# Whole 4 MB weight strips and one output tile at a time in the two big projections of an eight-core transformer layer

## The reference

```python
x = x + attn(layernorm(x))     # q = x@wq; k = x@wk; v = x@wv; causal softmax(q k / sqrt(128)) v; out @ wo
# second half, on x' = layernorm(x):
logits = x' @ W_router.T ; w = top-2 softmax weights over 8 experts
h = einsum('td,erd->ter', x', lora_A)
x = x + x' @ W_base.T + b_base + einsum('ter,eor,te->to', h, lora_B, w) * 2.0
```

## Time and profile before

| what | us |
|---|---|
| three runs | 4990.17, 5107.53, 5207.92 |
| their median | 5107.53 |
| profiled execution | 4992.11 |
| its span, slowest core (3) | 4990.3 |
| spans of the eight cores | 4944.2 to 4990.3 |
| first P4 weight transfer issued to first P4.5 read issued | 3183.10 to 3945.17, 762.1 |
| first P5 strip transfer issued to end | 4194.31 to 4990.3, 796.0 |

### The profile page before, as it was taken

One profiled execution on the slowest core, in us unless ns is written; L12 is line 12 of the kernel. 1 busy time (PEld: TensorE's weight loads), 2 busy tenths in 40 slices (PEclk: granted clock), 3 DMA queues, 4 the chain that ended last, 5 costly groups with the idle time before them and its releaser, 6 DMA issues.

```text
span 4990.3 us, 53555 instructions; the slowest of 8 cores (4944.2 to 4990.3 us)
## 1 busy us (share of the span) xinstructions
PE 3283.9 (66%) x16530; PEld 1520.3 (30%) x16530; DVE 1951.6 (39%) x3513; ACT 1796.4 (36%) x2024; POOL 159.5 (3%) x182
## 2 busy tenths in 40 slices
PE   3555555778787887878777777746655315646764
PEld 3455554332222222222222222222322212222322
DVE  4555554046556565656566777300000121000000
ACT  3555554036556565656556767300000020000000
POOL 0000000000000000000000000000000000000000
PEclk9888888999899999999898888877877657878887
DMA  6444443640111101110100000254444442444443
GB/s 181 158 164 166 165 165 104 62 38 9 18 18 18 18 9 17 18 18 9 17 9 1 1 1 1 41 98 88 84 94 89 116 93 32 87 94 82 87 90 77
DMA packets 260879, 328.70 MB, mean 66 GB/s; under 512 B 147712, under 2 KB 218496, under 8 KB 251264
## 3 DMA queue, kind: packets, MB, share of 16 engines
q0 software_dynamic: 212800, 106.97, 17.9%
q1 hardware_dynamic: 47808, 218.33, 13.0%
HBM read 398.66 MB, written 33.55 MB: 87 GB/s over the span
## 4 chain that ended last, share of the span: by engine, by line
PE 47%; DVE 25%; DMA 10%; issue 9%; ACT 7%; DVEq 1%; SPq 1%; ACTq 0%; POOL 0%; POOLq 0%
PE qps L633 10%; PE yps L708 9%; PE y2ps L989 9%; DVE at_tp L300 8%; PE vps L552 4%; DMA xsst<-xkv 4%; DMA x2r<-x2scr 4%; DVE at_sacc L323 4%; PE at_sps L242 3%; DVE at_tq L307 3%; DVE at_tr L308 3%; PE at_ppv L282 2%; PE ptx L505 2%; PE kps L566 2%; ACT xnTq L517 2%
## 5 line engine op out<-in xcount | busy, mean ns | idle before, releaser
L265 ACT ACTIVATE at_uring<-at_sps,bias 128x1024 bf16<-128x1024 f32 x896 | 945.5, 1115 | 42.2 <-DVE at_tp L300 33.0
L282 PE MATMUL at_ppv<-at_uring,Vs 128*128 128x512 bf16 x2304 | 706.0, 389 | 328.6 <-DVE at_uring L295 320.8
L242 PE MATMUL at_sps<-qT,kTs 128*128 128x512 bf16 x2304 | 698.7, 386 | 122.5 <-ACT at_uring L260 51.9
L708 PE MATMUL yps<-wost,qT 128*128 128x512 bf16 x2048 | 462.2, 390 | 271.1 <-DVE x2st L730 257.8
L989 PE MATMUL y2ps<-wbst,xnT 128*128 128x512 bf16 x2048 | 460.9, 389 | 265.7 <-DVE x3st L1034 252.7
L300 DVE TENSOR_TENSOR at_tp<-at_uring 128x512 bf16<-128x512 bf16 x1152 | 489.6, 425 | 298.4 <-ACT at_uring L260 175.3
L633 PE MATMUL qps<-xnT,wqbf 128*128 128x512 bf16 x2048 | 532.6, 426 | 41.1 <-issue 27.6
L552 PE MATMUL vps<-wkvbf,xnTq 128*128 128x128 bf16 x2048 | 216.6, 301 | 371.6 <-ACT Vs L575 347.8
L199 DVE RECIPROCAL at_sinvb<-at_sden 128x512 f32<-128x512 f32 x64 | 214.6, 3353 | 523.2 <-ACT at_sden L193 523.2
L282 PEld LDWEIGHTS at_ppv<-at_uring,Vs 128*128 128x128 bf16 x2304 | 214.7, 97 | 637.1 <-issue 400.9
L708 PEld LDWEIGHTS yps<-wost,qT 128*128 128x128 bf16 x2048 | 204.2, 100 | 530.1 <-issue 301.1
(11 more groups left out here) (97 smaller groups left out, 2218.3 us busy)
## 6 DMA issues: line engine op xcount, KB each, us to landing
xst<-xkv SPq DMA_DIRECT2D x64, 2048.0 KB, 9.6
wqbf<-wq POOLq DMA_DIRECT2D x32, 1024.0 KB, 12.1
wost<-wo POOLq DMA_DIRECT2D x64, 512.0 KB, 5.6
wbst<-wbT POOLq DMA_DIRECT2D x64, 512.0 KB, 5.5
xsst<-xkv SPq DMA_DIRECT2D x64, 256.0 KB, 3.3
x2scr<-x2st SPq DMA_DIRECT2D x64, 256.0 KB, 2.3
x2rd<-x2scr SPq DMA_DIRECT2D x8, 2048.0 KB, 8.2
x2r<-x2scr SPq DMA_DIRECT2D x64, 256.0 KB, 3.4
```

Source lines behind the costliest of these rows:

```text
L242: ins = t.matmul(sps[bi % 2][:, (jj - j0) * 512:(jj - j0 + 1) * 512], kT[:, jj * 128:(jj + 1) * 128], qslice(g, k), start=True, stop=True)
L265: ins = s.activation(u_t(gj, b), sps[bi % 2][:, 0:b * 512], AF.Exp, bias=bias10[:], scale=SCALE)
L282: ins = t.matmul(ppv[ei % 2][:], V[:, jj * 128:(jj + 1) * 128], u_t(gj0 + jj), start=(jj == 0), stop=(jj == nj - 1))
L708: ins = t.matmul(yps[tt][:], rawT4[:, tt, ic * 128:(ic + 1) * 128], wost[gq % 3][:, ic4:ic4 + 1, :].rearrange("p a n -> p (a n)"), start=( ...
```

## The change

Both big projections turn their loops inside out. A strip's weights come as one transfer of [128, 32, 512] (4 MB as bf16, 8 MB read) into one of two strip buffers. In P4 the two buffers are the two halves of `xnT`, which is not read between the last query projection and P4.5. In P5 they are two new tiles `ws5` on the right; to make room, `kT` and `V` are released after attention and most small tiles of P5's first part are released before its second. Then, for each row tile, one tensor event runs all 32 chunks (in P5 the bias and the low-rank matmul too, 34) into one of only four PSUM banks, and waits for the strip's transfer and for the add four tiles back. A tile's add now waits for that tile's matmuls alone. A strip's transfer waits for the last matmul event two strips back. The residual loads, the adds and the stores keep their form and their order on SP and DVE. P4.5's first copies into `xnT` also wait for the last P4 matmul. `xn2T` is another name for `xnT`.

P4 (P5 has the same form):

```diff
-        wost = [p4.enter_context(nc.sbuf_tensor(f"wost{i}", [128, 4, 512], BF16, side="right")) for i in range(3)]
+        ws4 = [xnT[:, i * 16384:(i + 1) * 16384].rearrange("p (q o) -> p q o", q=32)
+               for i in range(2)]
...
-        yps = [p4ps.enter_context(nc.psum_tensor(f"yps{i}", [128, 512], F32)) for i in range(8)]
+        NB4 = 4
+        yps = [p4ps.enter_context(nc.psum_tensor(f"yps{i}", [128, 512], F32)) for i in range(NB4)]
...
         for os_ in range(8):
-            for icq in range(8):
-                gq = os_ * 8 + icq
-                w = []
-                if gq >= 3:
-                    pq = gq - 3
-                    w.append(ev_ymm[(pq // 8, (pq % 8) * 4 + 3)])
-                ev_wo[(os_, icq)] = sched.event("gpsimd", ... wost[gq % 3][:] <- wo piece ...)
-                for ic4 in range(4):
-                    ic = icq * 4 + ic4
-                    w = [ev_wo[(os_, icq)]]
-                    if ic == 0 and os_ >= 1:
-                        w.extend(ev_yev[(os_ - 1, tt)] for tt in range(8))
-                    def em_y(t, ic=ic, ic4=ic4, gq=gq):
-                        for tt in range(8):
-                            ins = t.matmul(yps[tt][:], rawT4[:, tt, ic * 128:(ic + 1) * 128],
-                                wost[gq % 3][:, ic4:ic4 + 1, :]..., start=(ic == 0), stop=(ic == 31))
+            w = []
+            if os_ >= 2:
+                w.append(ev_ymm[(os_ - 2, 7)])
+            else:
+                w.extend(p3t_tensor)
+            ev_w4[os_] = sched.event("gpsimd", lambda g, os_=os_: g.dma_start(
+                    ws4[os_ % 2], wor[:, :, os_ * 512:(os_ + 1) * 512]), ...)
             for tt in range(8):
                 j = os_ * 8 + tt
+                w = [ev_w4[os_]]
+                if j >= NB4:
+                    w.append(ev_yev[((j - NB4) // 8, (j - NB4) % 8)])
+                def em_y(t, os_=os_, tt=tt, j=j):
+                    for ic in range(32):
+                        ins = t.matmul(yps[j % NB4][:], rawT4[:, tt, ic * 128:(ic + 1) * 128],
+                            xnT[:, (os_ % 2) * 16384 + ic * 512:(os_ % 2) * 16384 + (ic + 1) * 512],
+                            start=(ic == 0), stop=(ic == 31))
+                    return ins
+                ev_ymm[(os_, tt)] = sched.event("tensor", em_y, waits=w)
...
-                w = [ev_ymm[(os_, 31)], ev_xs[(os_, tt)]]
+                w = [ev_ymm[(os_, tt)], ev_xs[(os_, tt)]]
```

More of the change, by code:

```diff
@@ L685, in build_nc @@
         ev_x2w = {}
+        p3t_tensor = [e for e in p3_tail if e.sem == "tensor"]
         for os_ in range(8):
-            for icq in range(8):
-                gq = os_ * 8 + icq
-                w = []
-                if gq >= 3:
-                    pq = gq - 3
-                    w.append(ev_ymm[(pq // 8, (pq % 8) * 4 + 3)])
[L693 to L699, removed]
-                for ic4 in range(4):
-                    ic = icq * 4 + ic4
-                    w = [ev_wo[(os_, icq)]]
-                    if ic == 0 and os_ >= 1:
-                        w.extend(ev_yev[(os_ - 1, tt)] for tt in range(8))
-                    def em_y(t, ic=ic, ic4=ic4, gq=gq):
-                        for tt in range(8):
[L708 to L714, removed]
@@ L741, in build_nc @@
         qscope.close()
+        xn2T = xnT
         p45 = contextlib.ExitStack()
@@ L947, in build_nc @@
         p5ps1.close()
+        p5m.close()
         p5b = contextlib.ExitStack()
-        wbst = [p5b.enter_context(nc.sbuf_tensor(f"wbst{i}", [128, 4, 512], BF16, side="right")) for i in range(3)]
+        ws5 = [p5b.enter_context(nc.sbuf_tensor(f"ws5_{i}", [128, 32, 512], BF16, side="right")) for i in range(2)]
         wbstb = [p5b.enter_context(nc.sbuf_tensor(f"wbstb{i}", [128, 512], BF16, side="right")) for i in range(2)]
@@ L967, in build_nc @@
         for os_ in range(8):
[L968 to L994, removed]
             w = []
             if os_ >= 2:
-                w.append(ev_b5d[os_ - 2])
+                w.append(ev_y2[(os_ - 2, 7)])
+            ev_w5[os_] = sched.event(
+                "gpsimd",
+                lambda g, os_=os_: g.dma_start(
+                    ws5[os_ % 2][:], wbr[:, 0:32, os_ * 512:(os_ + 1) * 512]),
+                waits=w, inc=16, sem=f"c_wb{os_ % 2}")
+            w = []
+            if os_ >= 2:
+                w.append(ev_y2[(os_ - 2, 7)])
             ev_wb1[os_] = sched.event(
@@ L1001, in build_nc, with em_y2 @@
                 waits=w, inc=16, sem=f"c_wbb{os_ % 2}")
[L1003 to L1017, removed]
-            ev_lora[os_] = sched.event("tensor", em_lora, waits=[ev_b5, ev_hw, ev_bb])
             for tt in range(8):
                 j = os_ * 8 + tt
+                w = [ev_w5[os_], ev_wb1[os_]]
+                if j == 0:
+                    w.extend([ev_hw, ev_bb, ev_oc])
+                if j >= NB5:
+                    w.append(ev_y2ev[((j - NB5) // 8, (j - NB5) % 8)])
+                def em_y2(t, os_=os_, tt=tt, j=j):
+                    for dc in range(32):
+                        t.matmul(y2ps[j % NB5][:],
+                                 xn2T[:, dc * 1024 + tt * 128:dc * 1024 + (tt + 1) * 128],
+                                 ws5[os_ % 2][:, dc:dc + 1, :].rearrange("p a n -> p (a n)"),
+                                 start=(dc == 0), stop=False)
+                    t.matmul(y2ps[j % NB5][:], onechunk[:], wbstb[os_ % 2][:],
+                             start=False, stop=False)
+                    return t.matmul(y2ps[j % NB5][:], h_wT[:, tt * 128:(tt + 1) * 128],
+                                    bbf[:, os_ * 512:(os_ + 1) * 512],
+                                    start=False, stop=True)
+                ev_y2[(os_, tt)] = sched.event("tensor", em_y2, waits=w)
                 w = []
```

92 lines of the change are left out of this document (53 added, 39 removed).

## The result

| what | us |
|---|---|
| kernel before, median (lowest) of its ten runs | 5002.94 (4990.17) |
| changed kernel, median (lowest to highest) of its ten runs | 4441.17 (4436.96 to 4708.73) |
| ratio to the kernel before, 95% interval | 0.8882, 0.8871 to 0.8894 |
| forecast | 4418, range 4380 to 4650 |
| profiled execution used below | 4439.93, span 4438.4 |

The change makes the kernel 11.2% faster. The forecast was 23 us under the median.

A forecast was written before the change was run, and what follows sets the result against it. The bound was taken as the exposed latency of eight loads and adds between strips. Lead-in, matmuls and tail gave P4 479.0 and P5 505.3 us, saving 573.8 from 4992.1: 4418 us, range 4380 to 4650.

The forecast's parts named there:

- What bounds the kernel: P4 and P5: PE pauses 257.8 and 252.7 us for eight serial residual loads and adds after all banks fill.
- The streams: Matmuls without pauses, 0.216 us apart: 445.4 us in P4 and 471.7 in P5, cold starts saved.
- The tails: End of P4 and P5: only the last tile's drain, add, issue and store remain, 3.6 us each.
- The lead-ins: Start of P4 and P5: the first matmul waits for a whole strip, taken as 30 us in each stage.
- my bounds of 24.7 and 44.7: Lead-in limits in us: strip alone at 209 GB/s, or landing together with the second strip, each plus 4.6 to start.
- the 36 us: Lead-in worked out from the two `wqbf` transfers, where the first came at 0.8 of the whole.
- The add chain: P4 and P5 adds: 7.5 us a step while a strip lands, 3 us of lag, costed at nothing.
- The rival in which this chain sets the pace: Every load and add step takes 7.5 us, 51 us come back: 4469 us; chance 0.06.
- The clock: Rival: the clock does not hold in the unpaused P4 and P5 streams; at 0.90, 102 us more, 4520; chance 0.13.
- the 218 us: Spread of the three earlier runs, highest above lowest, added to 4418 for the range's upper side: 4636.
- The rivals of late strips: P4 and P5 strips land partly late, 65 us each: 4595, chance 0.05; or set the end, 98.4 us each: 5129, 0.03.
- the last two: Rivals: strips set the end, slower by 2.7%, 5129 us, chance 0.03; restructuring moves nothing, 4992 us, chance 0.01.

The follow-up runs named there:

- barrier_late: Changed kernel with 8 banks and the old add waits, each later strip issued only after the adds of the strip whose buffer it takes: 5043 to 5046 us, ratio 1.0078.
- prefetching kernel: Changed kernel with P4's first two strips issued during attention and P5's first during P4's last strip: median 4375.41 us, ratio 0.8757 to the kernel before.
- barrier: Changed kernel with 8 banks and the old waits (adds wait for the strip's last tile, next strip for all adds): 5179.8 and 5188.7 us, ratio 1.0378.

## Why the prediction was right, and what it missed

**What bounds the kernel: right.** The pauses were the serial adds behind the full set of banks. Putting the old waits back, with the strips kept out of the pauses, costs 603 us (barrier_late). Transfer size and loop order bring nothing by themselves: with them and the old waits the kernel is no faster than before.

**The streams: right.** P4's matmuls run from 3221.40 to the last add's start less 0.3, 450.7 us against 445.4 forecast, of which 4.2 are waits for adds. P5's take 472.1 against 471.7. The spacing of 0.216 us read from P2 holds with 32 and 34 matmuls in a row, through every strip border.

**The tails: right.** P4's is 3675.22 - 3672.39 = 2.8 us after the last add's start, plus 0.3 of drain, where 3.6 was forecast; P5's last 4.6 us, from the end of its matmuls to the end, are 1 us over.

**The lead-ins: the mis-sized term.** 30 us forecast for each stage, 38.7 and 41.3 measured on the slowest core. That is 20 of the 23 us. Both lie inside my bounds of 24.7 and 44.7, but the reasoning between them failed: I took the rate of 209 GB/s from core 3 without looking at what its neighbour did just then, and charged the excess to the core's own second strip alone. The runs show that two neighbouring cores loading together write some 160 GB/s each (157 on core 0 in 3190 to 3221, 159 on core 1 in 3186 to 3205). At that rate 4.19 MB take 26 us, 31 with the 4.6 to start, and this is when the slowest core had them (31.2). The lower rate beside a loading neighbour, a cause that the forecast did not have, thus explains 6.5 us over the 24.7; by the reckoning under the held-back strips most of it is the neighbour's first strip, which the run with the second strips held back left in place. The other 7.5 us, in which 1.2 MB of the second strip were written too, may be the own queue after all: the 36 us that I worked out for such a pair from the earlier trace rows, and then went below, was the nearer figure. In the kernel before, core 2 had issued its three pieces (1.5 MB) at 3175.40, 8 us ahead, and its rate was down from 202 GB/s in 3182 to 3184 to 57 in 3184 to 3190, so the two hardly met. With 4 MB each, 31.2 us of writing on core 0, they did.

The rest: P4's matmul waits and spacing add 5 us, and the stretch between the stages took 245.3 us instead of 249.1. So P4 and P5 came 26 us over the forecast, and 4 us of that came back by luck, in a stretch costed as unchanged.

**The add chain: right in price, wrong in size.** I gave a step 7.5 us while a strip lands, and 3 us of lag in all. The chain on core 0 shows the loads of three tiles in a row, and steps of 12.2, 9.4 and 7.7 us between the adds:

```profile
3336.89 0.70 DVE x2st L731
...
3338.07 10.90 DMA xsst<-xkv
3349.13 0.70 DVE x2st L731
3350.31 8.08 DMA xsst<-xkv
3358.55 0.70 DVE x2st L731
3359.73 6.39 DMA xsst<-xkv
...
3366.28 0.70 DVE x2st L731
```

Against 6.9 us for a tile that is 8.7 us of lag, three times what I said, and DVE waited for a load before 51 of 64 adds. It stayed free because the banks hold it and the loads of the later tiles take 3 to 5 us. The rival in which this chain sets the pace was nearer than 0.06 suggests in mechanism, but worth only 4 us here. In the prefetching kernel, where a strip lands in P4's last strip too, the same lag shows at the stage's end and costs 8 us there.

**The other rivals.** The clock held in this profile: all eight cores have 1.00 in 3240 to 3640, inside streams of 445 and 472 us. It did not in the execution of 4708.73 us (see the last section), which lies above the range, as that of 4662.97 does: the 218 us that I allowed for such a run, read from the kernel before, were too few. That rival was costed at two prices: 4520 is worked out from the 0.90 of the earlier trace rows; the higher one in the range rests on no row and no run. What the runs showed in its place is 1.00 on all eight cores in 3240 to 3640 and in 3990 to 4390 of one profile, and 0.81 in dense stretches of the execution of 4708.73 us. The rivals of late strips fell: a strip landed 35.2 us (median) after its issue in P4 and 30.5 in P5, well under the 55 and 59 us that there are. The chance of faster by over 2%, 0.95, does not quite follow from the chances given: all but the last two make 0.96.

## What to carry to other kernels

When all banks of a stage fill together, count the pause as the number of tiles times the latency of one load and one add, not as their busy time: here 8 x 4.5 = 36 us, with DVE busy for 5.39 of them. Finishing tiles one after the other into two banks hid it here, and more banks bought nothing (4438.2 and 4439.5 us with two, a median of 4441.17 with four), with each load issued a tile ahead. A larger transfer has a price at the start of the stage, here 27 to 43 us for a 4 MB strip where three pieces of 512 KB took 7.1, so issue the first one in the stage before, into whatever that stage has finished with, and look at what it slows down at that stage's end (8 us here). Before taking a transfer rate from a trace, look at what the neighbouring core moved in the same microseconds (205 GB/s here became some 160), and keep large transfers out of the moments in which small ones are waited for, which was worth some 140 us between the two kernels with the old barrier.

## What the runs showed of the hardware

A core wrote more slowly while its neighbour loaded too. Core 1 of the changed kernel writes its 4 MB casting transfer at 205 GB/s while core 0 is quiet (3179 to 3185) and at 159 when both load (3186 to 3205); core 0 has 157 (3190 to 3221). The other cores that start first fall likewise, in windows of 3 us: core 3 from 208 (3188 to 3191) to 162 (3194 to 3197), with core 2's issue at 3185.61, core 4 from 204 (3185 to 3188) to 161 (3191 to 3194), with core 5's at 3187.39, and core 6 from 205 (3185 to 3188) to 151 (3191 to 3194), with core 7's at 3180.93, each core by its own times. With two strips queued on each core, the first strip of P4 is ready after 27 to 31 us on the core that starts first and after 38 to 41 on the other; with one on each, after 27 to 29 and 30 to 33. Two bytes are read here for each one written, so 160 GB/s each is, by estimate, some 640 GB/s read by the pair, and core 1's 205 alone some 410. What it is that the two cores share, no run shows.

A 256 KB residual load (issue to landing) takes 3.3 us in the median and 6.2 at most in the P4 of the kernel before (core 3). While a 4 MB transfer of the same core lands it takes up to 12 us (11.93 in the pause of barrier shown above; the longest of P4 on that core is 12.5).

In the profile taken first of the changed kernel, at 4708.73 us, the granted clock over long dense stretches is 0.81, neither 1.00 nor the 0.50 at which the kernel before begins a burst (core 3, 3283 to 3287, 1.00 from 3288), and every matmul is slower. Core 6, P4, two windows:

```profile
3400.00:3500.00 100.00, 99.38 (x376) 41.43 (x381) 7.61 (x11) 0.00 (x0) 3.35 (x2) 0.81 0.72 137
3500.00:3600.00 100.00, 99.29 (x375) 41.40 (x382) 8.99 (x13) 0.00 (x0) 1.67 (x1) 0.81 0.54 113
```

Some 382 weight loads, one for each matmul, start in 100 us instead of 464 (a few matmul records of this core are missing), and a matmul takes 437 ns where it took 379. Dense streams alone do not bring the 0.81: in the profile at full clock all eight cores ran dense at 1.00 for 400 us (3240 to 3640). Nor did a whole die have it together: from 3650 to 3750 and again from 4150 to 4550 of their times cores 0 and 1 had 1.00 while cores 2 and 3 of the same die had 0.81, PE full on all four (core 0, then core 2):

```profile
4150.00:4550.00 400.00, 398.05 (x1818) 181.32 (x1853) 38.04 (x55) 0.00 (x0) 13.44 (x12) 1.00 0.70 140
```
```profile
4150.00:4550.00 400.00, 400.00 (x1525) 165.70 (x1524) 31.13 (x45) 0.00 (x0) 13.44 (x12) 0.81 0.60 120
```

Cores 4 and 5 changed together as well, at other times than 6 and 7: both 1.00 in 3500 to 3600, where 6 and 7 had 0.81, then 0.81 in 3700 to 3750 and 1.00 in 4450 to 4550, where 6 and 7 had 0.94. What decides was not tried.
